# Second attention of a hybrid block: the recurrent state kept per pair of heads, with a new step list

## What is computed

```
x = x + attn_a(norm(x))      # 16 heads of 64, causal linear attention with relu features
x = x + ffn(norm(x))         # rows quantised to int8 steps, times a quantised 512x512 matrix
x = x + attn_b(norm(x))      # below
x = x + ffn(norm(x))
```

```
q, k = rope(x @ q_w.T), rope(x @ k_w.T)            # per head 32 wide
q_r = einsum('bthd,hrd->bthr', q, Wq)              # 16 ranks per head, k_r likewise
g   = sigmoid(x @ g_w.T + g_b)
M   = M * decay + outer(g_t * k_t * scale, v_t)    # per head a state of 16 x 32
y_t = q_t @ M                                      # per head 32 wide
out = layernorm(x + Y @ out_w.T + out_b) * ln_g + ln_b
```

## Time and profile before

| what | value |
|---|---|
| median of three executions | 3481.64 us |
| the profiled execution | 3485.35 us |
| its span, first to last instruction | 3483.5 us |
| granted TensorE clock, mean over the span | 0.989 |
| setup, until the first transpose of chunk 0 | 117.3 us |
| instructions | 102125 |

### The profile page before, as it was taken

The page is one execution under the profiler, slowest core; times in us unless marked ns, Lnnn a source line. Parts: engine busy times, 40 slices in busy tenths (PEclk is TensorE's granted clock), DMA queues, the critical chain, the costliest instruction groups (busy, mean ns, idle before and its releaser), DMA issues.

```text
span 3483.5 us, 102125 instructions
## 1 busy us (share of the span) xinstructions
PE 3323.8 (95%) x44370; PEld 2560.1 (73%) x44498; DVE 2151.4 (62%) x4673; ACT 622.4 (18%) x1112; POOL 1071.5 (31%) x1374
## 2 busy tenths in 40 slices
PE   1599999999999999999999999999999999999995
PEld 1477777777777777777777777777777777777774
DVE  7455666666666666666566666666666666666664
ACT  2011111111111111111111111111111111111111
POOL 0022333333333333333233333332333333323333
PEclk9899999999999999999999999999999999999998
DMA  4100000000000000000000000000000000000000
GB/s 153 37 7 19 16 12 19 16 15 15 19 16 12 19 16 12 19 16 12 18 16 12 19 16 12 19 16 18 12 19 16 12 19 16 12 19 16 12 15 12
DMA packets 43816, 67.95 MB, mean 20 GB/s; under 512 B 13344, under 2 KB 21664, under 8 KB 43424
## 3 DMA queue, kind: packets, MB, share of 16 engines
q1 hardware_dynamic: 43424, 61.62, 5.8%
HBM read 44.83 MB, written 16.78 MB: 18 GB/s over the span
## 4 chain that ended last, share of the span: by engine, by line
PE 95%; DVE 3%; issue 1%; ACT 1%; POOL 0%; DMA 0%; DVEq 0%; SPq 0%; POOLq 0%; ACTq 0%
PE bank L564 19%; PE bank L565 19%; PE bank L566 19%; PE bank L531 7%; PE bank L814 6%; PE bank L627 4%; PE bank L653 4%; PE bank L710 3%; PE bank L775 2%; PE bank L640 2%; PE bank L667 2%; PE bank L796 2%; PE bank L758 2%; PE bank L749 2%; PE bank L785 2%; PE bank L806 2%
## 5 line engine op out<-in xcount | busy, mean ns | idle before, releaser
L564 PE MATMUL bank<-xaT_hi,wq_hi 128*128 128x128 f16 x2048 | 358.7, 220 | 1.7 <-DVE xaT_lo L1068 1.7
L566 PE MATMUL bank<-xaT_hi,wq_lo 128*128 128x128 f16 x2048 | 357.5, 220 | 0.0
L565 PE MATMUL bank<-xaT_lo,wq_hi 128*128 128x128 f16 x2048 | 357.4, 220 | 0.0
L564 PE MATMUL bank<-xaT_hi,wk_hi 128*128 128x128 f16 x2048 | 356.7, 220 | 0.0
L566 PE MATMUL bank<-xaT_hi,wk_lo 128*128 128x128 f16 x2048 | 356.6, 220 | 0.0
L565 PE MATMUL bank<-xaT_lo,wk_hi 128*128 128x128 f16 x2048 | 356.6, 220 | 0.0
L469 POOL TENSOR_TENSOR var_eps_o<-mean_var_o,eps 128x1 f32<-128x1 f32 x64 | 12.1, 189 | 767.7 <-DVE mean_var_o L1049 767.7
L814 PE MATMUL bank<-wout,turn_q 128*128 128x512 f32 x512 | 233.9, 600 | 2.1 <-ACT turn_q L923 2.1
L1224 DVE TENSOR_TENSOR work<-bank,causal 128x512 f32<-128x512 f32 x256 | 159.0, 684 | 105.0 <-PE bank L775 105.0
L564 PEld LDWEIGHTS bank<-xaT_hi,wq_hi 128*128 128x128 f16 x2048 | 200.5, 98 | 29.4 <-issue 14.1
L483 POOL TENSOR_TENSOR xwb<-xwa,xf 128x512 f32<-128x512 f32 x64 | 81.1, 1267 | 440.5 <-DVE xf L1168 440.5
(11 more groups left out here) (212 smaller groups left out, 9236.9 us busy)
## 6 DMA issues: line engine op xcount, KB each, us to landing
xin<-in_L_attn_a_x SPq DMA_DIRECT2D x64, 256.0 KB, 2.6
out<-xf SPq DMA_DIRECT2D x64, 256.0 KB, 2.0
table<-in_tables SPq DMA_DIRECT2D x64, 192.5 KB, 2.4
work<-in_L_attn_a_Wq SPq DMA_DIRECT2D x1, 2048.0 KB, 7.7
work<-in_L_attn_a_Wk SPq DMA_DIRECT2D x1, 2048.0 KB, 14.8
work<-in_L_attn_a_Wv SPq DMA_DIRECT2D x1, 2048.0 KB, 8.0
work<-in_L_attn_a_Wo SPq DMA_DIRECT2D x1, 2048.0 KB, 8.4
work<-in_L_attn_b_q_w SPq DMA_DIRECT2D x1, 1024.0 KB, 4.8
```

The costliest lines, as they stand in the source:

```text
L564: nc.tensor.matmul(o, a[0], b[0], start=first, stop=False)
L565: nc.tensor.matmul(o, a[0], b[1], start=False, stop=False)
L566: return nc.tensor.matmul(o, a[1], b[0], start=False, stop=last)
```

## The change

The state of the second attention is stored per pair of heads: for each half of the heads 128 rows (four pairs, 32 rows each) by 64 columns (the two heads of the pair, 32 each). The mask `own_head` shrinks to 64 columns and now keeps the head's own 32 columns by whether the head is odd or even. `ub` becomes eight products on column strips 32 wide, 64 columns each; `ys` becomes eight products of 32 rows by 64 columns. They go to two banks, `y0` for the even blocks of y and `y1` for the odd ones; `yb` adds to the same two, and `y_e` is two copies. `sb` now takes the two banks of y besides its own four. The tables `ORDER`, `BANK` and `COUNTS` are replaced as a whole: lags now go up to 4, so there are 68 slots, 0 to 3 and 64 to 67 of them partly filled.

```diff
-ORDER = [("qb_a", 3), ("o0_e", 1), ("aT0", 1), ("qr", 3), ("qT0", 2), ("kb_a", 3), ("s1_e", 1), ("aT0_h", 1),
...
+ORDER = [("ld_x", 0), ("y_e", 4), ("na_st", 0), ("s0_e", 1), ("na_rs", 0), ("na_ap", 0), ("nf0_ap", 2), ("kt0", 1),
+         ("out", 4), ("ld_t", 3), ("nb_rs", 3), ("kt0_e", 1), ("kt1", 1), ("v1", 1), ("out_e", 4), ("no_st", 4),
...
-         "wo": "wo0", "y": "ys", "sb0": "sb", "sb1": "sb", "sb2": "sb", "sb3": "sb"}
+         "wo": "wo0", "y0": "sb", "y1": "sb", "sb0": "sb", "sb1": "sb", "sb2": "sb", "sb3": "sb"}
...
-        own_head = sb("own_head", [P, HALF_H, DB])
+        own_head = sb("own_head", [P, 2 * DB])
-        state_b = sb("state_b", [P, 2, 2 * P])
+        state_b = sb("state_b", [P, 2, 2 * DB])
...
             def sb_(c):
                 four = [c.take(f"sb{l}") for l in range(4)]
+                c.take("y0")
+                c.take("y1")
+                c.wait(b_ready, c.count(1))
                 c.done("kr")
                 c.done("qr")
...
             def ys(c):
-                bank, _ = c.take("y")
-                c.done("qr")
-                c.wait(b_ready, c.count(1))
-                for b in range(BB):
-                    nc.tensor.matmul(bank[:, tile(b)], state_b[:, b // 2, tile(b % 2)], qh[:, b // 2, :],
-                                     start=b == 0, stop=False, skip_group_check=True)
+                two = [ps[BANK["y0"]], ps[BANK["y1"]]]
+                for j in range(2):
+                    for g in range(4):
+                        nc.tensor.matmul(two[g // 2][64 * (g % 2):64 * (g % 2) + 64, tile(j)],
+                                         state_b[32 * g:32 * g + 32, j, :], qh[32 * g:32 * g + 32, j, :],
+                                         start=j == 0, stop=False, skip_group_check=True)
...
             def ub(c):
...
                 for j in range(2):
-                    last = nc.tensor.matmul(bank[:, 256 * j:256 * j + 256], khat[:, tile(j)],
-                                            vbs[:, 256 * j:256 * j + 256], start=True, stop=True)
+                    for g in range(4):
+                        h = 8 * j + 2 * g
+                        last = nc.tensor.matmul(bank[32 * g:32 * g + 32, 64 * j:64 * j + 64],
+                                                khat[:, h * R:(h + 2) * R], vbs[:, h * DB:(h + 2) * DB],
+                                                start=True, stop=True, skip_group_check=True)
                 last.then_inc(f, 1)
...
             def y_e(c):
-                bank, e = c.read("y")
-                nc.scalar.activation(yT, four(bank), ACT.Copy).then_inc(e, 1)
+                for odd in range(2):
+                    bank, e = c.read(f"y{odd}")
+                    nc.scalar.activation(yT.rearrange("p (j two) t -> p two j t", two=2)[:, odd, :, :],
+                                         bank[:, 0:256].rearrange("p (j t) -> p j t", j=2), ACT.Copy).then_inc(e, 1)
```

More of the change, by code:

```diff
@@ L38 @@
 MAGIC = 1.5 * 2.0 ** 23
-ORDER = [("qb_a", 3), ("o0_e", 1), ("aT0", 1), ("qr", 3), ("qT0", 2), ("kb_a", 3), ("s1_e", 1), ("aT0_h", 1),
-         ("ld_x", 0), ("na_st", 0), ("v1_e", 1), ("gb_k", 3), ("qr_e", 3), ("na_rs", 0), ("kr", 3), ("kr_e", 3),
[4 rows of a table removed]
-         ("bias", 1), ("qk0_e", 0), ("out", 3), ("qk1_e", 0), ("ld_t", 2), ("v0", 0), ("out_e", 3),
-         ("no_st", 3), ("no_ap", 3), ("no_rs", 3), ("ub_e", 3), ("nb_rs", 2), ("qk2", 0), ("no_f", 3),
[7 rows of a table removed]
+ORDER = [("ld_x", 0), ("y_e", 4), ("na_st", 0), ("s0_e", 1), ("na_rs", 0), ("na_ap", 0), ("nf0_ap", 2), ("kt0", 1),
+         ("out", 4), ("ld_t", 3), ("nb_rs", 3), ("kt0_e", 1), ("kt1", 1), ("v1", 1), ("out_e", 4), ("no_st", 4),
[12 rows of a table added]
+         ("ub_e", 3)]
 LAG = dict(ORDER)
@@ L60 @@
 MAX_LAG = max(LAG.values())
[L63 removed]
[3 rows of a table removed]
+BANK = {"xTa": 2, "v0": 7, "v1": 1, "qk0": 2, "qk1": 5, "qk2": 6, "qk3": 2, "kt0": 6, "s0a": 2, "s0b": 3, "o0a": 4,
[3 rows of a table added]
 BANKS = 8
 TAKES = {"s0a": "s0", "s0b": "s0", "s1a": "s1", "s1b": "s1", "o0a": "s0", "o0b": "s0", "o1a": "s1", "o1b": "s1",
[L69 removed]
+         "wo": "wo0", "y0": "sb", "y1": "sb", "sb0": "sb", "sb1": "sb", "sb2": "sb", "sb3": "sb"}
 SETUP_UNITS = 23
@@ L335, in hybrid_kernel @@
         s_exp = sem("exp_done")
+        s_parity = sem("head_parity_ready")
         rank_ready = sem("rank_ready")
@@ L793, in yb @@
                 for b in range(BB):
+                    bank, f, _ = two[b % 2]
                     for l in range(HPB):
                         h = HPB * b + l
-                        last = nc.tensor.matmul(bank[l * DB:(l + 1) * DB, tile(b)], vbs[:, h * DB:(h + 1) * DB],
-                                                scb[:, h % 8 // 2, 2 * (h // 8) + h % 2, :], start=False, stop=b == BB - 1,
+                        last = nc.tensor.matmul(bank[l * DB:(l + 1) * DB, tile(b // 2)], vbs[:, h * DB:(h + 1) * DB],
+                                                scb[:, h % 8 // 2, 2 * (h // 8) + h % 2, :], start=False, stop=b > 1,
                                                 skip_group_check=True)
-                last.then_inc(f, 1)
+                    if b > 1:
+                        last.then_inc(f, 1)
             def ub(c):
@@ L811, in out_ @@
                 bank, f = c.take("out")
-                c.done("y")
+                c.done("y0")
+                c.done("y1")
                 for k in range(KD):
@@ L964, in spread_ranks @@
                                             block16.rearrange("p (h two) i -> p h two i", two=2)[:, :, odd, 0],
-                                            AX_X, ALU.add)
+                                            AX_X, ALU.add).then_inc(s_parity, 1)
+                dve.wait_ge(s_parity, 2)
+                for odd in range(2):
+                    h = slice(odd * DB, (odd + 1) * DB)
+                    nc.vector.tensor_scalar(own_head[:, h], own_head[:, h], odd_even[:, odd:odd + 1], None, ALU.mult)
                 for w in range(2):
```

51 lines of the change are left out of this document (21 added, 30 removed), and 51 rows, old and new, of tables (BANK, COUNTS, ORDER).

## The result

| | before | after |
|---|---|---|
| median of the runs, us | 3482.94 (3481.57 to 3484.91) | 3379.51 (3377.39 to 3381.18) |
| profiled execution, us | 3485.4 | 3381.18 |
| its span, us | 3483.5 | 3379.4 |
| full slot, us (x to x, 59 slots) | 51.65 | 50.20 |
| span less 64 full slots, us | 177.7 | 166.6 |

The ratio is 0.9702, with a 95% interval from 0.9685 to 0.9719: 103 us less. The forecast was 3395 us, 16 us too high; the result lies half a microsecond inside the low end of the range. The direction and the size of the main terms were right. Two others were wrong, the loss at the loop's jump and the two ends of the kernel, and they are what most of the experiments are about.

What follows compares the result with a forecast made beforehand. PE's work was taken as the bound. Terms summed to -1.33 us a slot, -85 us over 64 chunks, plus -2 at the ends: 3398 us profiled, 3395 us forecast for the median, range 3379 to 3427.

Steps and rivals of the forecast that it cites:

- the two ends: Pipeline filling and emptying: -5 us and +3 us, together -2 us, ends -10 and +8.
- `ys`: 16 small issues, four abreast, replace 8 single ones: 0.89 to 0.44 us, -0.45 us a slot.
- `ub`: 16 issues of 64 columns on four column strips: 0.89 to 0.24 us, -0.65 us a slot.
- changes of shape, 12 to 10: PE's array changes shape 10 times a slot instead of 12, 0.14 us each: -0.28 us a slot.
- loop registers: On PE's queue in two slots, 61 register instructions instead of 23: +0.05 us a slot, ends 0 and 0.27.
- The bank rule: Rival: `ys` tiles sharing a bank take turns, 0.45 us a slot not gained, 3424 us; chance 0.14.
- the margins at `sb`, `qk3` and `o1`: Evictions and masks finish before PE needs them in full slots, with over 1 us to spare at each.
- a new wait: Rival: in full slots some reader comes 0.6 us beyond its margin, 38 us, 3433 us; chance 0.10.
- six banks of `sb`: Rival: DVE reaches `sb` late, PE waits 2.1 us every slot, 134 us, 3529 us; chance 0.04.
- the 0.16 us of idle time: PE's idle time per full slot before the change, taken to contain the present loop register instructions.
- Filling: First slots: a v projection and `s0` now stand between PE's former waits for DVE's evictions; -5 us.
- The emptying: Last rounds with lag 4: 133 us for about 79 us of PE work, lost 54 us instead of 51, +3.

Runs made afterwards that it cites:

- experiment 1: New step list and banks, but the state's wide tiles of the kernel before for `ys` and `ub`; 3447.84 us, ratio 0.9885 against the kernel before.
- experiments 2: Kernel before with its old list and banks, but small tiles and `ys` moved directly ahead of `ub`; 3428.49 us, ratio 0.9831.
- experiment 4: Kernel before with `qb` in bank 7 instead of bank 6, which `kb` also has; 3483.05 us, ratio 1.000.
- Experiment 9: Kernel before with its loop's end moved from behind `v1` to between `out` and `v0`; 3479.48 us, ratio 0.9985.

## Why the prediction came out as it did

The slot was to shrink by 1.33 us and shrank by 1.453.

| term, us a slot | predicted | measured |
|---|---|---|
| `ys` | -0.45 | -0.44 |
| `ub` | -0.65 | -0.64 |
| changes of shape, 12 to 10 | -0.28 | -0.23 |
| loop registers | +0.05 | 0 |
| loss at the jump | not in the sum | -0.14 |

- **`ys`: right.** The step went from 0.995 us to 0.598, with +0.011 on `wo1` (experiment 1 against after): -0.39 together. The 0.995 are eight rounds (0.89) and one change of shape out of `sb`; in the 0.598 are four rounds (0.44), so the rounds give -0.44. The other 0.06 us are what the change of shape costs that the small tiles add.
- **The bank rule.** The trace does not bear it out for this kernel: the issues of row strips 0 and 1 go to one bank, those of 2 and 3 to another, and 16 issues take 0.60 us, with four starts 7 ns apart; one after the other in pairs they would need 8 x 0.111 = 0.89. The rule of the Trainium skill, "TensorEngine Tiling (Array Packing)", section "Gotcha 1: PSUM Pressure", would have given 3424 us. One limit: the two strips that share a bank here also lie on different columns of the array. Row strips on the same columns with one bank were not tried.
- **`ub`: right.** -0.709 for the step, -0.025 on `yb`, +0.093 on `v0`. The 16 issues start 0.0155 us apart on average (in fours, 7 ns apart), 0.248 in all, in line with `so`, and not the 0.40 us that would follow, as an estimate, from about 25 ns between starts (the Trainium skill, "TensorE: Matmul & The Clock Gate", section "Wait — 56ns, not 53.3ns?").
- **Changes of shape: right in direction, a little too dear.** Off the jump, the list alone (experiment 1) takes the slot from 51.51 to 51.23, -0.29, but for three changes: 12 become nine there, and the small `ys` brings the tenth back for 0.06. That leaves -0.23 for the two, where 0.14 each was summed; a change cost 0.095 to 0.107 us. That the list needs no new wait anywhere is shown by PE's idle time of 0.00 in the full slots; the margins at `sb`, `qk3` and `o1` held, and the rivals "a new wait" and "six banks of `sb`" did not occur.
- **Registers: wrong, and with them the idle time.** The step that failed reads "the present ones are within the 0.16 us of idle time". The prediction took that idle time as a rest that stays, perhaps grows with the registers. It was neither: two thirds of it were unrecorded matmuls, and what was really lost was lost at the jump, 0.28 us in each slot that holds it and nothing in the others, as the lengths of the slots in the trace before (51.51 and 51.80) would have told. 61 register instructions for 23 cost nothing: slots with the jump and slots without take 50.20 us alike. The new list happens to put the jump where both stops are covered, and that is worth 8 to 9 us (27 jumps at 0.284 us, or 0.139 x 64) against this trace of the kernel before. That is luck, as nothing in the prediction asked where the jump would fall; and experiments 2 and 4 lost only 0.07 and 0.04 us at the old place, so how much of it another execution of the kernel before would show is not settled. Experiment 9 gets nearly the same on the old list by nothing but moving the jump (5.9 us in the medians, interval 1.7 to 8.4).
- **The two ends: the size was off.** Predicted -2 us together, measured -10.3. Filling: idle time up to slot 4 went from 9.5 to 1.6 us, -7.9 where I had -5. The emptying was to cost +3; what is left for it is -2.4. I carried the old pace of 37 to 38 us from `out` to `out` over to a list with another order; it became 36.8, 32.5 and 34.9. The granted clock in the emptying was alike, 0.86 and 0.85, but some 5 us of the -10.3 may be chance (experiment 4). What paces the emptying was not taken apart: the waits of 5.6 us for POOL ahead of `qr` that the old list has there are gone from the new one, in experiment 1 as well as in the changed kernel.

So of the 17 us by which the profiled execution was below its forecast (3398 against 3381.2), 8 are in the slots, 8 at the ends, 1 in the setup, which two traces of the same program can differ by. Both missed terms went the same way and took the result to the edge of the range: that it is still inside owes half a microsecond to luck.

No version beat the changed kernel. Inside the slots PE is idle 0.00 us, so only less work on PE or fewer changes of shape, at 0.107 us a slot each, 7 us a kernel, would help there.

## What to carry to other kernels

Look at the lengths of single iterations before you call an average idle time small and harmless: here every second slot was 0.28 us longer, and that pointed to the cause. When a hardware loop's body is rotated or its list replaced, the place of the jump is an edit of its own: have long issues queued ahead of it and some 4 us of few, long issues behind it (as far as these lists show), and compare slots with the jump to slots without. A chain of many short issues next to it cost 2 us a round here, up to 59 us in this kernel, with every wait in the code unchanged. Narrow products side by side on strips are worth their changes of shape (0.107 us each) where they cut the rounds by more; put steps of one shape next to each other.
